# A last stage with sixteen columns, each token in one: tokens sorted on chip into 43 gathered tiles

## The reference, cut to what matters

```
x = x + tanh(g_ffn[1]) * L1_ffn(layernorm(x))

def L1_ffn(x):                                  # x: 32 x 112 tokens, D = 256; C = 16 columns, N = 64
    similarity = l2norm(x) . l2norm(col_emb)                      # per token, 16
    gate       = sigmoid(gelu(x @ gate_w1 + gate_b1) @ gate_w2 + gate_b2)
    logits     = similarity + gate
    mask       = one-hot of the largest logit                     # k = max(1, int(16 * 0.05)) = 1
    weights    = mask * softmax(logits)
    cols       = gelu(x @ W_cols[c] + b_cols[c]) * weights[c]     # for all 16 c
    y          = concat(cols) @ proj_w + proj_b + x
    return (y - mean(y)) * rsqrt(var(y) + 1e-5) * ln_g + ln_b
```

## Time and profile before

| | us |
|---|---|
| median of three runs (1379.34 to 1384.43) | 1380.5 |
| span of the profiled execution | 1385.6 |
| PE busy | 1304.1 (94%) |
| DVE busy | 968.4 (70%) |
| ACT busy | 678.4 (49%) |
| POOL busy | 528.1 (38%) |

### The profile page before, as it was taken

One profiled execution on the slowest core, in us unless ns is written; L12 is line 12 of the kernel. 1 busy time (PEld: TensorE's weight loads), 2 busy tenths in 40 slices (PEclk: granted clock), 3 DMA queues, 4 the chain that ended last, 5 costly groups with the idle time before them and its releaser, 6 DMA issues. The chain is left out here.

```text
span 1385.6 us, 32665 instructions
## 1 busy us (share of the span) xinstructions
PE 1304.1 (94%) x12672; PEld 924.2 (67%) x12672; DVE 968.4 (70%) x1641; ACT 678.4 (49%) x1447; POOL 528.1 (38%) x781
## 2 busy tenths in 40 slices
PE   4789999999999985999999999999998899999996
PEld 4565777877787763666777677667775575555555
DVE  7776666567656768888888888888885553454445
ACT  5854211221122124787787778877876452232220
POOL 1428888888880008333333333333320552000000
PEclk9999999999999996999999999999999699999999
DMA  8515454545451009566655556666540000000000
GB/s 222 127 42 159 133 166 135 170 135 165 134 160 42 35 4 189 94 102 101 99 93 92 91 94 102 102 100 100 93 80 2 1 1 1 14 14 26 13 13 26
DMA packets 92814, 120.28 MB, mean 87 GB/s; under 512 B 7426, under 2 KB 78939, under 8 KB 90388
## 3 DMA queue, kind: packets, MB, share of 16 engines
q1 hardware_dynamic: 83476, 87.85, 31.9%
q0 software_dynamic: 9216, 30.73, 8.2%
HBM read 96.45 MB, written 22.10 MB: 86 GB/s over the span
## 5 line engine op out<-in xcount | busy, mean ns | idle before, releaser
L1251 DVE TENSOR_REDUCE s_neg_max<-banks 112x3 bf16<-112x1461 f32 (+1 forms) x192 | 290.2, 1511 | 45.0 <-PE banks L1367 44.8
L1165 ACT ACTIVATE s_prob<-banks 128x448 f32<-128x448 f32 x512 | 272.3, 544 | 91.6 <-PE banks L1393 76.5
L702 DVE TENSOR_TENSOR s_m<-banks,s_base 128x512 f32<-128x512 f32 x256 | 161.1, 683 | 99.2 <-PE banks L856 98.9
L1393 PE MATMUL banks<-s_q_t,s_k_t 112*128 112x112 bf16 x2048 | 186.5, 215 | 1.1 <-ACT s_prob L1165 1.0
L1393 PEld LDWEIGHTS banks<-s_q_t,s_k_t 112*128 112x128 bf16 x2048 | 124.2, 98 | 72.5 <-issue 50.5
L856 PE MATMUL banks<-s_gate_sel,s_tw 64*128 64x256 f32 x1024 | 130.8, 394 | 1.6 <-DVE s_m L702 1.5
L899 PE MATMUL banks<-s_m,s_act_t 128*112 128x256 f32 x512 | 128.2, 388 | 1.5
L1409 PE MATMUL banks<-s_prob,s_v 128*32 128x112 f32 (+1 forms) x4096 | 125.8, 263 | 0.7 <-ACT s_prob L1165 0.7
L881 PEld LDWEIGHTS banks<-s_x_t,s_m 128*128 128x128 f32 x1024 | 116.7, 192 | 10.6 <-issue 7.6
L881 PE MATMUL banks<-s_x_t,s_m 128*128 128x112 f32 x1024 | 122.4, 278 | 0.0
L1890 PE MATMUL banks<-s_proj,s_weighted 128*112 128x256 f32 x512 | 115.4, 380 | 0.0
(11 more groups left out here) (271 smaller groups left out, 2340.7 us busy)
## 6 DMA issues: line engine op xcount, KB each, us to landing
k_parts<-s_k_split POOLq DMA_DIRECT2D x64, 281.2 KB, 3.7
s_k_t<-k_parts SPq DMA_DIRECT2D x32, 562.5 KB, 7.9
s_tw<-in_tw SPq DMA_DIRECT2D x16, 1024.0 KB, 5.5
s_k_raw<-in_ctx_k POOLq DMA_DIRECT2D x64, 187.5 KB, 3.8
s_k_t<-k_parts SPq DMA_DIRECT2D x32, 375.0 KB, 5.3
s_v_raw<-in_ctx SPq DMA_DIRECT2D x32, 256.0 KB
s_src<-in_ctx SPq DMA_DIRECT2D x8, 896.0 KB, 16.2
s_k_t<-k_parts SPq DMA_DIRECT2D x32, 187.5 KB, 9.1
```

Source lines behind the costliest of these rows:

```text
L702: nc.vector.tensor_tensor(dst[:, :, :, rows_], got, base[:, :, rows_].unsqueeze(2).broadcast_to([P, 2, B, HR]), ALU.add).then_inc(S["merge ...
L1165: nc.scalar.activation(prob[t % 2][:, c, :], w.bank(SCORE + n % SRING, P, TILE), ACT.Exp, scale=DH ** -0.5).then_inc(S["exp_done"], 1)
L1251: nc.vector.tensor_reduce(neg_max[half][:, ROWS + first:ROWS + end, 0], w.banks[0:T, MAX:MAX + end - first, 0:NKEY], AX.X, ALU.max, negate ...
L1393: last = nc.tensor.matmul(w.bank(SCORE + n % SRING)[:, s * T:(s + 1) * T], k_t[k][0:ROWS_MAX, h, c * P:(c + 1) * P], q_t[k][0:ROWS_MAX, h, :],
```

## The change

In place of all sixteen columns for every token, each token is multiplied by its own column alone. The tokens are sorted by column into tiles of 128 slots, each tile of one column. A column's last tile may be part empty, so up to (3584 - 16) // 128 + 16 = 43 tiles can be needed, and always 43 are done.

- POOL adds `ln_b` and `proj_b` group by group, all before the sort, and SP stores both sums of each token, 2 KB, to `x_rows` in DRAM: sixteen transfers of 448 KB.
- DVE counts with a scan over the one-hot `hit`; PE turns the counts into ranks (three matmuls); DVE works out each token's slot, its tile and its place within; PE multiplies 32 one-hot pairs into a table with a token number and a weight for each slot; DVE unpacks it into `comes_from`, `goes_to` and `weight`, and the tiles' columns into `column_of`.
- For each tile n: POOL gathers its 128 rows from `x_rows` by an indirect transfer, five tiles ahead; SP reads the column's number into a register and copies the column's weights (64 KB) within SBUF into one of four buffers; PE turns the rows, ACT evacuates with `proj_b` taken off again, PE multiplies by 64 weights, ACT reads the column's number and applies the gelu with its bias, PE reads it and multiplies by the column's part of the projection; DVE scales by the weight and adds the residual, takes the statistics, and nine tiles later writes the result; POOL scatters it to the output by a second indirect transfer (empty slots point past the end and are skipped). Root and inverse are taken for eight tiles at once.
- The loop over tiles is written out, without a loop instruction; the weights are laid out by column; semaphores of stage 1 are cleared by POOL at the end of stage 3 and used again.

Its core:

```diff
@@ gate, setup of stage 3 and 4 @@
+SLOT_TILES = (B * T - C4) // P + C4
...
-        self.x_res = sb("x_res", [T, B, D])
+        self.x_all = sb("x_res", [P, B, D])
+        self.x_res = self.x_all[0:T]
...
+        self.x_rows = nc.dram_tensor("x_rows", (B * T, 2 * D), F32, kind="Internal").ap()
...
@@ stage3, POOL, behind its last turn @@
+                for signal in w.finished:
+                    pool.sem_clear(signal)
...
@@ stage4 @@
+    N_TILES, AHEAD4, LAG, SQRT_LAG = SLOT_TILES, 5, 9, 2
+    GROUP, SEMS, RING_W = 8, 8, 4
...
             def _(sp):
-                with sp.Fori(0, NG // 2) as i:
-                    for k in range(2):
-                        g = 2 * i + k
-                        sp.wait_ge(S["res_done"], nth(g))
-                        sp.dma_start(w.out[bass.ds(g * GB, GB)].rearrange("b t d -> t b d"), res[k][:]).then_inc(stored[k], 16)
...
+                for g in range(NG):
+                    rows_ = slice(g * GB, (g + 1) * GB)
+                    wait(sp, "x_biased", GB * (g + 1))
+                    sp.dma_start(rows_of[:, rows_, D:2 * D], w.x_res[:, rows_, :]).then_inc(rows_in, 16)
+                    wait(sp, "kept", GB * (g + 1))
+                    sp.dma_start(rows_of[:, rows_, 0:D], xn[:, rows_, :]).then_inc(rows_in, 16)
+                wait(sp, "columns_done", 1)
+                for n in range(N_TILES):
+                    wait(sp, "col_ps", n - RING_W + 1)
+                    c = sp.value_load(column_of[0:1, n:n + 1], min_val=0, max_val=C4 - 1)
+                    sp.dma_start(w_tile[n % RING_W][:], w_cols[:, :, bass.ds(c * N4, N4)]).then_inc(w_in[n % RING_W], 16)
...
             def _(pool):
-                add_ln(0, B // 2)
...
-                wait(pool, "wts_done", 1)
-                add_ln(B // 2, B)
+                for g in range(NG):
...
+                        nc.gpsimd.tensor_tensor(w.x_res[:, b, :], w.x_res[:, b, :], ln_b[:], ALU.add)\
+                            .then_inc(S["x_biased"], 1)
...
+                        nc.gpsimd.tensor_tensor(xn[:, b, :], xn[:, b, :], proj_b[:], ALU.add).then_inc(S["kept"], 1)
+                wait(pool, "in_tile_done", 1)
+                nc.gpsimd.tensor_tensor(carry[:, :, 0, :], in_tile[:], token[:].unsqueeze(2).broadcast_to([T, B, N_TILES]),
+                                        ALU.mult).then_inc(S["token_done"], 1)
+                def fetch(n):
+                    if n >= SEMS:
+                        pool.wait_ge(row_in[n % SEMS], 16 * (n // SEMS))
+                    if n >= RING4:
+                        pool.wait_ge(stored[n % SEMS], 16 * ((n - RING4) // SEMS + 1))
+                    nc.gpsimd.indirect_dma_start(row(n), None, w.x_rows[:, :],
+                                                 bass.IndirectOffsetOnAxis(ap=comes_from[:, n:n + 1], axis=0))\
+                        .then_inc(row_in[n % SEMS], 16)
+                def store(n):
+                    wait(pool, "res_done", n + 1)
+                    if n >= SEMS:
+                        pool.wait_ge(stored[n % SEMS], 16 * (n // SEMS))
+                    nc.gpsimd.indirect_dma_start(out_rows, bass.IndirectOffsetOnAxis(ap=goes_to[:, n:n + 1], axis=0), y_of(n),
+                                                 None, bounds_check=B * T - 1, oob_is_err=False)\
+                        .then_inc(stored[n % SEMS], 16)
+                pool.wait_ge(rows_in, 16 * 2 * NG)
+                wait(pool, "slots_done", 1)
+                for n in range(AHEAD4):
+                    fetch(n)
+                for n in range(N_TILES + LAG):
+                    if n + AHEAD4 < N_TILES:
+                        fetch(n + AHEAD4)
+                    if n >= LAG:
+                        store(n - LAG)
...
             def _(act):
-                        nc.scalar.activation(x_t[:, :, b * T:(b + 1) * T], got, ACT.Copy)
...
+                def evacuate_row(n):
+                    wait(act, "turned", n + 1)
+                    wait(act, "col_ps", n - 1)
+                    for kk in range(KD):
+                        last = nc.scalar.activation(x_tt[n % 2][:, kk, :], w.bank(n % 2)[:, kk * P:(kk + 1) * P],
+                                                    ACT.Identity, bias=neg_b[:, kk:kk + 1])
+                    last.then_inc(S["x_tt_done"], 1)
+                def gelu(n):
+                    c = act.value_load(column_of[0:1, n:n + 1], min_val=0, max_val=C4 - 1)
+                    wait(act, "col_ps", n + 1)
+                    wait(act, "y_ps", n - 1)
+                    nc.scalar.activation(hid_c[n % 2][:], w.bank(2 + n % 2, N4, P), ACT.Gelu,
+                                         bias=b_cols[:, bass.ds(c, 1)]).then_inc(S["gelu_done"], 1)
...
+                for n in range(N_TILES):
+                    if n + 1 < N_TILES:
+                        evacuate_row(n + 1)
+                    gelu(n)
+                    if n >= SQRT_LAG and group_end(n - SQRT_LAG):
+                        roots(n - SQRT_LAG)
...
             def _(dve):
+                nc.vector.tensor_tensor_scan(flat(cum), flat(keep), flat(hit), 0.0, ALU.mult, ALU.add)\
+                    .then_inc(S["cum_done"], 1)
...
+                wait(dve, "rank_ps", 1)
...
+                nc.vector.tensor_tensor(in_tile[:], steps[0:T, 0:N_TILES].unsqueeze(1).broadcast_to([T, B, N_TILES]),
+                                        tile_of[:].unsqueeze(2).broadcast_to([T, B, N_TILES]), ALU.is_equal)\
+                    .then_inc(S["in_tile_done"], 1)
...
+                for q in range(4):
+                    at = slice(q * 8, q * 8 + 8)
+                    nc.vector.tensor_tensor(spot[:, at, :], steps[0:T, 0:P].unsqueeze(1).broadcast_to([T, 8, P]),
+                                            within[:, at].unsqueeze(2).broadcast_to([T, 8, P]), ALU.is_equal)\
+                        .then_inc(S["spot_done"], 1)
...
+                nc.vector.tensor_scalar(column_of[:], column_f[:], float(C4 - 1), None, ALU.min).then_inc(S["columns_done"], 1)
+                wait(dve, "table_ps", 1)
...
+                def summed(n):
+                    wait(dve, "y_ps", n + 1)
+                    nc.vector.scalar_tensor_tensor(out=y_of(n), in0=w.bank(4 + n % 4, P, D), scalar=weight[:, n:n + 1],
+                                                   in1=y_of(n), op0=ALU.mult, op1=ALU.add).then_inc(S["summed"], 1)
...
+                for n in range(N_TILES + LAG):
+                    now, old = n < N_TILES, n >= LAG
+                    if now:
+                        summed(n)
+                    if old:
+                        centred(n - LAG)
+                    if now:
+                        stat(n)
+                    if old:
+                        finish(n - LAG)
+                    if now:
+                        mean_variance(n)
+                    if now and group_end(n):
+                        radicands(n)
+                    if n >= 1 and n - 1 < N_TILES and group_end(n - 1):
+                        inverses(n - 1)
...
             def _(pe):
+                wait(pe, "cum_done", 1)
+                nc.tensor.matmul(w.bank(1, P, C4), ones16[:], cum[:, :, B - 1], start=True, stop=True)
+                nc.tensor.matmul(w.bank(0, T, C4 * B), not_before[:], hit[:].rearrange("t c b -> t (c b)"), start=True, stop=False)
+                nc.tensor.matmul(w.bank(0, T, C4 * B), ones16[:, 0:T], cum[:].rearrange("t c b -> t (c b)"), start=False,
+                                 stop=True).then_inc(S["rank_ps"], 1)
...
+                def turn(n):
+                    pe.wait_ge(row_in[n % SEMS], 16 * (n // SEMS + 1))
+                    wait(pe, "x_tt_done", n - 1)
...
+                        last = nc.tensor.transpose(w.bank(n % 2)[:, kk * P:(kk + 1) * P], row(n)[:, kk * P:(kk + 1) * P],
+                                                   w.ident[:])
...
+                def column(n):
+                    wait(pe, "x_tt_done", n + 1)
+                    pe.wait_ge(w_in[n % RING_W], 16 * (n // RING_W + 1))
+                    wait(pe, "gelu_done", n - 1)
...
+                        last = nc.tensor.matmul(w.bank(2 + n % 2, N4, P), w_tile[n % RING_W][:, kk, :], x_tt[n % 2][:, kk, :],
+                                                start=(kk == 0), stop=(kk == KD - 1))
...
+                def output(n):
+                    c = pe.value_load(column_of[0:1, n:n + 1], min_val=0, max_val=C4 - 1)
+                    wait(pe, "gelu_done", n + 1)
+                    wait(pe, "summed", n - 3)
+                    nc.tensor.matmul(w.bank(4 + n % 4, P, D), hid_c[n % 2][:], proj[:, bass.ds(c * D, D)],
+                                     start=True, stop=True).then_inc(S["y_ps"], 1)
...
+                turn(0)
+                for n in range(N_TILES):
+                    if n + 1 < N_TILES:
+                        turn(n + 1)
+                    column(n)
+                    if n >= 1:
+                        output(n - 1)
+                output(N_TILES - 1)
```

(51 more changed lines are left out.)

335 lines of the change are left out of this document (134 added, 201 removed).

## The result

The changed kernel takes 1323.3 us (median of four runs, 1323.1 to 1324.4) against 1382.5 for the kernel before beside it: a ratio of 0.957, 95% interval 0.955 to 0.959. It is faster, inside the range, 37 us above the forecast of 1286.

What follows compares the result with a forecast made beforehand. PE bounds the kernel before; POOL's transfers were to set the changed loop's pace. 1180 to the first store + 83.5 + 27.5 = 1291 us span, 94.6 below 1385.6, so 1286 us in time; range 1256 to 1345.

Steps and rivals of the forecast that it cites:

- The choice: Before the sort: DVE finishes choosing each token's column at 1138.3 us, little moving before; POOL's reordered additions cost nothing.
- The sort, 17.9 us: From the choice to known slots: a DVE chain, slots near 1156.2, with PE's 32 small matmuls hidden beside the compares.
- PE's price, 0.65 us at 2.4 GHz and 1.3 at 1.2: Loop over tiles: PE's matmuls per tile, four of 128 columns and one of 256; 1.3 us was counted.
- The register load, 1 us: Loop: PE loads a column number before its last matmul; 1 us, beside earlier matmuls, making PE 2.3 us a tile.
- POOL, 2 x 1.44 = 2.88: Loop: two indirect transfers a tile, 1.44 us each, make POOL set the pace at 2.88 us, DVE close behind.
- The early turns at 1.6 us: After the first sum: eight turns with three of DVE's five operations, near 1.6 us each; first store near 1180.
- The fill, 7.5 us: From slots to first sum: first gather lands, is turned, evacuated, multiplied, put through gelu and projected; first sum near 1164.
- Between the first store and the last gather, 29 turns: Steady loop: 29 turns at POOL's pace of 2.88 us, 83.5 us in the sum.
- The tail: After the last gather: fourteen more stores beside DVE's last turns, then the last scatter, 1.4 + 3.2; 27.5 us in all.
- The loop's clock "well under 1": Sign of being right: PE's granted clock in the loop well under 1, as PE waits more than it works.
- The rivals: POOL held until landing, 1472 us, chance 0.06; POOL and DVE taking turns, 1366, 0.06; transfer engines bounding, 1313, 0.12.
- The rule quoted against the change: GpSimd's transfer descriptors wait while DVE holds the shared port pair; at 3.1 us for each of 86, span 1426 us.

Runs made afterwards that it cites:

- e2: The changed kernel with the scatter of every second tile left out: 1319.4 us.
- e3: The changed kernel with the loop's column and projection matmuls in bf16: 1307.6 us.
- e6: The changed kernel without POOL's addition of the projection's bias for the second half of the batches (16 additions): 1316.9 us.
- e10: The changed kernel with e3's and e4's edits, the carry's batch part on DVE, and POOL's last 8 additions put behind the prefix sum: 1294.3 us.
- e4: The changed kernel with the sort's 32 table matmuls in bf16, the token's number split into batch and row: 1302.4 us.
- e5: The changed kernel with 128 useless matmuls keeping TensorE busy in the sort's three waits: 1313.4 us.
- e8: e2's kernel with TensorE's register load gone as well, every tile taking column 0's projection: 1317.7 us.
- e7: The changed kernel without SyncE's 43 column-weight transfers and its register loads, every tile using column 0's weights in place: 1321.6 us.

## Why the prediction was right, and where it was not

The direction held for the reason given: 43 tiles in place of sixteen columns. Of the 94.6 us forecast 59.2 came (1382.5 to 1323.3). What bounds the loop failed: the prediction named POOL, with PE's work beside it, and it is PE (e2, e3). The span is 30.5 us above the sum; 6.9 more are in the step to the time (1380.5 is 5.1 below its span, 1323.3 is 1.8 above).

| step | predicted | measured | off by |
|---|---|---|---|
| choice done | 1138.3 | 1143.0 | +4.7 |
| from there to slots | 17.9 | 28.3 | +10.4 |
| slots to first sum | 7.8 | 10.4 | +2.6 |
| first sum to first store | 16 | 27.7 | +11.7 |
| first store to last gather | 83.5 | 77.2 | -6.3 |
| last gather to the span's end | 27.5 | 34.9 | +7.4 |

- *The choice, "before that point little moves"*: failed. POOL's additions were counted as many as before and early enough, and so they were; but they now lie beside DVE's gate addition: 4.7 us (e6). The one-hot as transposed bf16 added 1.7 (2.38 against 0.69); against that the add began 1.6 us earlier than before.
- *The sort, 17.9 us*: the passes of DVE came out as priced. The matmuls "run beside the compares" didn't: 13.9 us instead of 3.5 to 7, of which 8.8 were waited for, and 2.4 us went to the first spot beside POOL's product (1.22 us in e10, where POOL has no work there). e4 and e5 both take most of the 8.8 away.
- *PE's price, 0.65 us at 2.4 GHz and 1.3 at 1.2*: the term that was most wrong, and with it the bound. It is 1.58 (e4) and 2.81. The prediction took the earlier trace rows for 512 matmuls; the kernel has eight for each of 32 batches, 256, so an fp32 matmul stands in two records there, as 42 stand in 84 after. The 0.22 us of the earlier trace rows is half a matmul; the same error halved the table. Counted right, the rows give 2 x 0.11 + 4 x 0.11 + 2 x 0.22 = 1.1 us, 2.2 at 1.2 GHz; the pieces of the turn are 0.62 + 1.04 + 1.15 = 2.81, and where the other 0.6 us come from stays open. At 2.4 GHz, 0.216 us for 256 columns are two clocks a column, so four in two records. By the Trainium skill (FP8 and Floating Point Precision, "TensorE Precision Notes") true FP32 takes four passes; the rows agree.
- *The register load, 1 us, "beside earlier matmuls"*: the second half was right, and with it the 1 us should not have been in the sum: 0.00 (e8).
- *POOL, 2 x 1.44 = 2.88*: 2.6 with the gaps. It came near 2.81 only because two wrong prices met: POOL's too high, PE's too low. The early turns at 1.6 us were wrong with PE's price: eight at 2.8 make 9.6 of the 11.7.
- *The fill, 7.5 us*: the price was for one tile alone. In PE's queue the first projection stands behind the turns of the next two tiles and the second tile's column product; the chain has 4.6 us of PE there.
- *Between the first store and the last gather, 29 turns*: 28 were left, as POOL had issued 15 gathers by then, and they took 77.2 us.
- *The tail*: the last stores come 1.3 us apart (1.44 priced), but 7.3 us follow the last of them instead of a landing of 3.2, and from the last sum to the last scatter's end there are 15.9 us instead of 12.9.
- *The loop's clock "well under 1"*: 0.50, but by luck. The reason given was that PE would wait more than it works; it was busy for 120.92 of 126.00 us. Why the clock stayed there is open (e4, e5).
- *The rivals*: POOL isn't held to a landing (0.94 to 1.13 us), nor do its transfers take turns with DVE's operations, and the copies are hidden (e7). The rule quoted against the change, 620 ns grown to 3100, isn't seen in any of the 86 transfers. But of another section of that page of the Trainium skill (SBUF — State Buffer, "Who interferes with whom") the prediction used only the list of three operations. The Trainium skill also says there that a DVE instruction with two inputs in SBUF contends with a GpSimd instruction that reads SBUF; the add of 5.37 us and the spot of 3.52 agree, and both were in the sum at their price alone.

## What to carry to other kernels

Count records against the matmuls in the code before taking a duration from them: a group of 512 may be 256 in two passes. When work becomes a chain of short turns, price each engine's turn at the lower clock, for the bound can stay with the engine that the change relieved. And look what another engine does beside a step that is priced alone: the 64 additions cost nothing by their own count, yet 4.7 us by their place.

## What the runs showed that was not expected

- After the last scatter on POOL 7.3 us pass to the end of the span, with no engine busy; with 22 scatters instead of 43 it is 5.6. No view shows what is done in them; that fewer scatters make them shorter is all that the runs show.
- The same loop ran at two paces in one run, 1.58 and 2.81 us, as the granted clock was 1.00 or 0.50; PE busy nearly throughout at either.
- A DVE operation beside POOL's additions either waited for all eight of them (5.37 us) or took turns with them (1.25 us, and POOL's then took 1.17 instead of 0.72).
